# Five layer norms done in halves of 128 positions, in a chain of six layers on one core

## What is computed

```
y   = x + neighbourhood_attention(x) * gate(x)            # layer 0
a   = layernorm(y) * ln_g + ln_b                          # norm 1
xn  = group_norm(a);  t1 = xn + attention(xn)             # layer 1, softmax over 256 positions
x2  = layernorm(t1)                                       # norm 2
t2  = t1 + dilated_attention(x2)                          # layer 2
x3  = layernorm(t2)                                       # norm 3
t3  = t2 + top2_of_8_experts(x3)                          # layer 3
x4  = layernorm(t3)                                       # norm 4
t4  = t3 + causal_attention(x4)                           # layer 4
x5  = layernorm(t4)                                       # norm 5
out = t4 + lstm(x5)                                       # layer 5, 256 steps in sequence
layernorm(z) = (z - mean(z)) / sqrt(var(z) + 1e-5)        # over the 64 channels of a position
```

## Time and profile before

| | |
|---|---|
| Median of 3 runs | 422.7 us (421.83 to 422.84) |
| The profiled execution, its own time | 422.28 us |
| Its span, first to last instruction | 420.4 us |
| Busy: PE, DVE, ACT | 70%, 61%, 50% of the span |
| Mean granted TensorE clock | 0.635 of 2.4 GHz |
| LSTM loop, first matmul to the transposes of its result | 118.3 to 417.0 us |

### The profile page before, as it was taken

One profiled execution on the slowest core, in us unless ns is written; L12 is line 12 of the kernel. 1 busy time (PEld: TensorE's weight loads), 2 busy tenths in 40 slices (PEclk: granted clock), 3 DMA queues, 4 the chain that ended last, 5 costly groups with the idle time before them and its releaser, 6 DMA issues.

```text
span 420.4 us, 11844 instructions
## 1 busy us (share of the span) xinstructions
PE 292.6 (70%) x3273; PEld 224.5 (53%) x3278; DVE 257.7 (61%) x2308; ACT 212.3 (50%) x1172; POOL 12.1 (3%) x22
## 2 busy tenths in 40 slices
PE   6899889989875666666556666665566666656663
PEld 2466347743455555555555555555555555555553
DVE  1786454655356666666666666666666666666665
ACT  2687253254455555555555555555555555555552
POOL 5410000000000000000000000000000000000000
PEclk9999999799975555555555555555555555555555
DMA  7500000000000000000000000000000000000000
GB/s 278 229 3 2 0 2 1 0 2 0 0 3 2 0 0 0 0 0 0 0 0 0 0 0 0 0 0 0 0 0 0 0 0 0 0 0 0 0 0 12
DMA packets 2972, 5.60 MB, mean 13 GB/s; under 512 B 1424, under 2 KB 1680, under 8 KB 2960
## 3 DMA queue, kind: packets, MB, share of 16 engines
q1 hardware_dynamic: 2672, 5.09, 3.3%
q10 hardware_dynamic: 288, 0.36, 0.2%
HBM read 5.32 MB, written 0.13 MB: 13 GB/s over the span
## 4 chain that ended last, share of the span: by engine, by line
ACT 38%; PE 37%; DVE 14%; issue 9%; DMA 1%; SPq 0%; DVEq 0%
ACT bank L383 20%; PE bank L665 17%; ACT gi L371 10%; DVE ha L949 6%; DVE terms_a L949 4%; ACT bank L373 4%; PE bank L424 2%; PE bank L446 2%; PE bank L394 2%; PE bank L435 1%; PE bank L597 1%; PE bank L558 1%; PE bank L609 1%; DMA cst<-in_const 1%; PE bank L479 1%
## 5 line engine op out<-in xcount | busy, mean ns | idle before, releaser
L665 PE MATMUL bank<-ha,vparts 128*128 128x1 f16 x1536 | 96.0, 169 | 110.8 <-DVE ha L949 110.8
L665 PEld LDWEIGHTS bank<-ha,vparts 128*128 128x128 f16 x1536 | 75.1, 107 | 133.7 <-DVE ha L949 133.7
L371 ACT ACTIVATE gi<-bank 128x1 f32<-128x1 f32 x256 | 43.8, 171 | 145.4 <-PE bank L665 145.4
L383 ACT ACTIVATE bank<-bank,hc,gi 128x2 f32<-128x2 f32 x256 | 83.5, 326 | 0.0
L946 DVE TENSOR_SCALAR go<-go 128x1 f32<-128x1 f32 x256 | 39.4, 154 | 66.3 <-ACT go L377 66.3
L665 PE MATMUL bank<-hb,vparts 128*128 128x1 f16 x768 | 76.4, 165 | 0.0
L665 PEld LDWEIGHTS bank<-hb,vparts 128*128 128x128 f16 x768 | 60.7, 104 | 0.0
L949 DVE CUSTOM_DVE_ANT_0 terms_a<-bank,go 128x3 f32<-128x3 f32 x256 | 41.2, 161 | 29.2 <-ACT bank L383 0.2
L661 PE MATMUL bank<-x,w5s 128*128 (+1 forms) x198 | 56.0, 358 | 0.1
L474 PE MATMUL bank<-ones,w5s 128*128 128x8 f32 x198 | 55.6, 355 | 0.0
L955 DVE SCALAR_TENSOR_TENSOR cell<-bank,gi,hc 128x1 f32<-128x1 f32 x256 | 54.7, 214 | 0.0
(11 more groups left out here) (215 smaller groups left out, 293.6 us busy)
## 6 DMA issues: line engine op xcount, KB each, us to landing
rel<-in_positions SPq DMA_DIRECT2D x4, 352.0 KB, 5.4
w3s<-in_w SPq DMA_DIRECT2D x1, 804.0 KB, 9.6
ltr<-in_later SPq DMA_DIRECT2D x1, 709.0 KB, 7.3
w2s<-in_w SPq DMA_DIRECT2D x1, 640.0 KB, 8.4
w5s<-in_w SPq DMA_DIRECT2D x1, 576.0 KB, 10.6
w0s<-in_w ACTq DMA_DIRECT2D x1, 336.0 KB, 4.0
w1s<-in_w SPq DMA_DIRECT2D x1, 256.0 KB, 7.5
w4s<-in_w SPq DMA_DIRECT2D x1, 192.0 KB, 10.5
```

Source lines behind the costliest of these rows:

```text
L371: act.activation(gi[:], bank[pre + 1][:, at:at + 1], ACT.Sigmoid, scale=1.0 / PRE)
L383: act.activation(tc_ends, gt.broadcast_to([P, 2]), ACT.Tanh, scale=gi[:], bias=hc[:]).then_inc(on("tanh_c"), 1)
L665: return mm(bank[3 * parity + k][:, at:at + 1], vparts[:, part, k], h, start=False, stop=False, skip_group_check=True)
```

## The change

Every step of a norm is issued for columns 0 to 127 and then for columns 128 to 255, each with a semaphore count of its own, and the two halves have separate banks. The copy to `rsw` goes; in place of the transposes, four f32 matmuls take the reciprocals themselves as the stationary operand, repeated 64 times by a broadcast, against the identity. The sources are made in halves. Seven of the eight `keep_clock` matmuls of norms 1 to 4, and all of norm 5's, go. Norm 5's `b_part`s move ahead of it, in place of one of the fillers there, and the first `x_part`s wait for the first half of x5 alone, the loop for both. After the group norm's square root, ACT asks for the Exp table. The experts' gate takes the first half of x3 as soon as it is there.

```diff
-        dif_bank, var_bank, rs_bank = ({n: bank[3 * (n == 5) + i] for n in range(1, 6)} for i in (0, 1, 2))
+        norm_bank, var_bank = ({n: (bank[3 * (n == 5) + i], bank[3 * (n == 5) + i + 1]) for n in range(1, 6)} for i in (0, 2))
+        half = [slice(h * P, (h + 1) * P) for h in range(HALVES)]
...
                 ask_table(ACT.Sqrt)
+                first = HALVES * (n - 1)
+                for h in range(HALVES):
+                    act.wait_ge(on("dif_mm"), first + h + 1)
+                    act.activation(sq[:, half[h]], norm_bank[n][h][:, 0:P], ACT.Square).then_inc(on("squares"), 1)
                 act.wait_ge(on("eps_set"), 2)
+                for h in range(HALVES):
+                    act.wait_ge(on("var_mm"), first + h + 1)
+                    act.activation(sd[:, h], var_bank[n][h][:, 0:B], ACT.Sqrt, bias=epsc[:, 0:1]).then_inc(on("root"), 1)
...
             act.activation(gtm[:, 2:3], gtm[:, 1:2], ACT.Sqrt, scale=-1.0, bias=epsc[:, 1:2]).then_inc(on("gsd"), 1)
+            ask_table(ACT.Exp)
...
+            def norm(n, src, made):
+                first = HALVES * (n - 1)
+                for h in range(HALVES):
+                    pe.wait_ge(on(made), h + 1)
+                    mm(norm_bank[n][h][:, 0:P], c("centre"), src[:, half[h]], start=True, stop=True).then_inc(on("dif_mm"), 1)
+                for h in range(HALVES):
+                    pe.wait_ge(on("squares"), first + h + 1)
+                    mm(var_bank[n][h][:, 0:B], sq[:, half[h]], c("means"), start=True, stop=True).then_inc(on("var_mm"), 1)
+                for h in range(HALVES):
+                    pe.wait_ge(on("rs"), first + h + 1)
+                    pe.wait_ge(on("dif"), first + h + 1)
+                    for b in range(B):
+                        m = mm(norm_bank[n][h][b * C:(b + 1) * C, 0:P], rs[:, h, b:b + 1].broadcast_to([P, C]),
+                               ident, start=True, stop=True)
+                    m.then_inc(on("rs_mm"), 1)
                 if n < 5:
+                    keep_clock(var_bank[n][0], 1)
...
             for h in range(HALVES):
+                pe.wait_ge(on("x3"), (h + 1) * B)
                 for b in range(B):
                     u = h * B + b
                     m = mm(bank[2][:, u * E:(u + 1) * E], x3[:, b, h * P:(h + 1) * P], cols(w3s, W3, "gate"),
...
-            keep_clock(bank[1], 4)
-            pe.wait_ge(on("t4"), 1)
+            keep_clock(bank[1], 3)
             pe.wait_ge(on("ub_scaled"), 2)
             pe.wait_ge(on("ones_set"), 1)
-            norm(5, t4[:])
+            for k in range(3):
+                b_part(0, k)
+            norm(5, t4, "t4")
...
             for k in (1, 0, 2):
                 x_part(0, k, 0)
+            pe.wait_ge(on("x5"), HALVES)
...
+            for h in half:
+                link(stt(out=pg[:, h], in0=bank[1][:, h], scalar=v("bp0"), in1=gate[:, h], op0=ALU.add, op1=ALU.mult))
+                tt(y0[:, h], pg[:, h], xf[:, h], ALU.add).then_inc(on("y0"), 1)
...
+                for h in range(HALVES):
+                    dve.wait_ge(on("squares"), first + h + 1)
+                    dve.tensor_copy(dif[:, half[h]], norm_bank[n][h][:, 0:P]).then_inc(on("dif"), 1)
+                for h in range(HALVES):
+                    dve.wait_ge(on("root"), first + h + 1)
+                    dve.reciprocal(rs[:, h], sd[:, h]).then_inc(on("rs"), 1)
...
+                for h in range(HALVES):
+                    dve.wait_ge(on("rs_mm"), first + h + 1)
+                    dve.wait_ge(on("dif"), first + h + 1)
+                    if n == 3:
+                        for b in range(B):
+                            r = slice(b * C, (b + 1) * C)
+                            tt(dst[r, b, half[h]], dif[r, half[h]], norm_bank[n][h][r, 0:P], ALU.mult).then_inc(on(done), 1)
+                    else:
+                        tt(dst[:, half[h]], dif[:, half[h]], norm_bank[n][h][:, 0:P], ALU.mult).then_inc(on(done), 1)
...
+            for h in half:
+                stt(out=t1[:, h], in0=bank[2][:, h], scalar=v("bp1"), in1=xn[:, h], op0=ALU.add, op1=ALU.add)\
+                    .then_inc(on("t1"), 1)
...
+            for i, h in enumerate(half):
+                tt(cc[:, h], bank[5][:, h], wsig[:, h], ALU.mult).then_inc(on("cc"), 1)
+                dve.wait_ge(on("cc"), 2 + i)
+                tt(t4[:, h], cc[:, h], cc2[:, h], ALU.add).then_inc(on("t4"), 1)
```

More of the change, by code:

```diff
@@ L126, in build @@
         sd, rs = sb("sd", [P, HALVES, B]), sb("rs", [P, HALVES, B])
-        rsw = sb("rsw", [P, HALVES, B, C])
         epsc = sb("epsc", [P, 2])
@@ L475, in b_part @@
                           start=True, stop=False, skip_group_check=True)
-            def norm(n, src):
-                mm(dif_bank[n][:, 0:N], c("centre"), src, start=True, stop=True).then_inc(on("dif_mm"), 1)
-                keep_clock(rs_bank[n], 2)
-                if n < 5:
[L482 to L501, removed]
-            keep_clock(bank[1], 4)
+            def norm(n, src, made):
[13 more added lines that the diff above has]
+                    m.then_inc(on("rs_mm"), 1)
+                if n < 5:
+                    keep_clock(var_bank[n][0], 1)
+            norm(1, y0, "y0")
+            keep_clock(bank[4], 4)
             pe.wait_ge(on("gst"), 1)
@@ L506, in _ @@
             mm(bank[2][:, 0:2], c("group"), gst[:], start=True, stop=True).then_inc(on("group_mm"), 1)
-            keep_clock(bank[1], 7)
+            keep_clock(bank[4], 7)
             pe.wait_ge(on("xn"), 1)
@@ L543, in _ @@
             keep_clock(bank[6], 2)
-            pe.wait_ge(on("t1"), 1)
-            norm(2, t1[:])
-            pe.wait_ge(on("x2"), 1)
+            norm(2, t1, "t1")
+            pe.wait_ge(on("x2"), HALVES)
             pe.wait_ge(on("w2_in"), 16)
@@ L580, in _ @@
             keep_clock(bank[2], 2)
-            pe.wait_ge(on("t2"), 1)
-            norm(3, t2[:])
-            pe.wait_ge(on("x3"), B)
+            norm(3, t2, "t2")
             pe.wait_ge(on("w3_in"), 16)
             for h in range(HALVES):
+                pe.wait_ge(on("x3"), (h + 1) * B)
                 for b in range(B):
@@ L639, in _ @@
             down(E - 1)
-            pe.wait_ge(on("t3"), 1)
-            norm(4, t3[:])
-            pe.wait_ge(on("x4"), 1)
+            norm(4, t3, "t3")
+            pe.wait_ge(on("x4"), HALVES)
             pe.wait_ge(on("w4_in"), 16)
@@ L764, in _ @@
             dve.wait_ge(on("gate"), 1)
-            link(stt(out=pg[:], in0=bank[1][:, 0:N], scalar=v("bp0"), in1=gate[:], op0=ALU.add, op1=ALU.mult))
-            tt(y0[:], pg[:], xf[:], ALU.add).then_inc(on("y0"), 1)
+            for h in half:
+                link(stt(out=pg[:, h], in0=bank[1][:, h], scalar=v("bp0"), in1=gate[:, h], op0=ALU.add, op1=ALU.mult))
+                tt(y0[:, h], pg[:, h], xf[:, h], ALU.add).then_inc(on("y0"), 1)
             def norm(n, dst, done):
[L771 to L777, removed]
+                first = HALVES * (n - 1)
+                for h in range(HALVES):
[4 more added lines that the diff above has]
+                    dve.reciprocal(rs[:, h], sd[:, h]).then_inc(on("rs"), 1)
@@ L789, in _ @@
+            norm(1, lno, "lno")
+            dve.wait_ge(on("lno"), HALVES)
             ts(t0[:], lno[:], v("lng"), v("lnb"), ALU.mult, ALU.add).then_inc(on("t0"), 1)
@@ L825, in _ @@
             dve.wait_ge(on("proj1_mm"), 1)
-            stt(out=t1[:], in0=bank[2][:, 0:N], scalar=v("bp1"), in1=xn[:], op0=ALU.add, op1=ALU.add)\
-                .then_inc(on("t1"), 1)
-            norm(2, x2[:], "x2")
+            for h in half:
+                stt(out=t1[:, h], in0=bank[2][:, h], scalar=v("bp1"), in1=xn[:, h], op0=ALU.add, op1=ALU.add)\
+                    .then_inc(on("t1"), 1)
+            norm(2, x2, "x2")
             for d in range(3):
@@ L871, in _ @@
             dve.wait_ge(on("proj2_mm"), 1)
-            stt(out=t2[:], in0=bank[6][:, 0:N], scalar=v("bp2"), in1=t1[:], op0=ALU.add, op1=ALU.add)\
-                .then_inc(on("t2"), 1)
-            norm(3, x3[:], "x3")
+            for h in half:
+                stt(out=t2[:, h], in0=bank[6][:, h], scalar=v("bp2"), in1=t1[:, h], op0=ALU.add, op1=ALU.add)\
+                    .then_inc(on("t2"), 1)
+            norm(3, x3, "x3")
             dve.wait_ge(on("gate_mm"), 1)
@@ L918, in _ @@
             dve.wait_ge(on("down_mm"), E)
-            tt(t3[:], bank[7][:, 0:N], t2[:], ALU.add).then_inc(on("t3"), 1)
-            norm(4, x4[:], "x4")
+            for h in half:
+                tt(t3[:, h], bank[7][:, h], t2[:, h], ALU.add).then_inc(on("t3"), 1)
+            norm(4, x4, "x4")
             dve.wait_ge(on("w4_in"), 16)
@@ L937, in _ @@
             dve.wait_ge(on("x5_zero"), 1)
-            norm(5, x5[:, 0:N], "x5")
+            norm(5, x5, "x5")
             split = "ha holds at most 11 bits by its grid, hb is rounded as a rest"
```

9 lines of the change are left out of this document (removed).

## The result

The changed kernel takes 416.74 us (median of 20 runs, 415.36 to 421.31) and the kernel before 421.89 us (median of 20, 421.00 to 423.54). The medians are 5.2 us apart. The ratio is that of the means of all runs (417.67 and 422.06) and not of the medians: 0.9896, with a 95% interval of 0.9874 to 0.9918: 1.0% faster, 4.4 us. The forecast was 417.9 us, within 415.9 to 420.9, and 4.8 us of gain.

A forecast was written before the change was run, and what follows sets the result against it. The kernel was taken as bound by its unchanged LSTM loop (298.7 us) and the 118 us of serial layers before it. Terms summed to 4.77 us off 422.28, 417.51, plus 0.42 to the median: 417.9 us, range 415.9 to 420.9.

The forecast's parts named there:

- The chain of a norm: Second half of a norm, from the source's end to the result's: 2.69 us, against 3.63 before.
- The savings of norms 1, 2, 4 and 5: Norms issued by halves save 0.57 us in norm 1, 0.77 in norm 2, 0.83 in norm 4, 0.91 in norm 5.
- the Exp table: Layer 1: the table load moves into ACT's idle time, so the Exps start earlier; 0.45 us saved.
- the gate's term: After norm 3: the first half's four gate records run under DVE's products, saving 0.46 us.
- norm 3's: Two products per half, one per image: 4.08 us becomes 3.30, saving 0.78; 1.24 with the gate.
- Layer 2: The stage from x2 to t2, with no instruction changed: 0 us saved.
- rival C: The clock's fall at 72.4 goes, values' projections and transposes run faster, about 2.5 us: 415.4 us; chance 0.08.
- Rival A: Without fillers the clock falls in the norms: 420.9 us with one fall (chance 0.09), 426 with a long one (0.04).
- single fall: One clock fall in the norms costs at most 3.4 us, about 3 where PE isn't always the bound: 420.9; chance 0.09.
- Rival B: The norms' halves don't overlap; only the copy's 0.32 per norm and the Exp table remain, 2.05 us: 420.2; chance 0.13.

The follow-up runs named there:

- exp_only: The kernel before, with only the Exp table asked for right after the group norm's square root: 421.39 us, ratio 0.9988.
- whole_bcast: The kernel before, norms whole and fillers kept, with 64-wide broadcast-reciprocal matmuls replacing copy and transposes: 421.91 us, ratio 1.0002.
- fill_3: The changed kernel with the fillers put back in norm 3 alone: 417.46 us, ratio 0.9886.
- no_fill: The kernel before, norms whole, with only the change's reduced fillers (one at the end of norms 1 to 4, none inside): 426.23 us, ratio 1.0105.
- rs_turn: The changed kernel with fillers in norms 1 to 4, but with the copy to rsw and the transposes, by halves: 417.31 us, ratio 0.9888.
- logit_fill: The changed kernel with fillers in norms 1 to 4 and four more among layer 2's logits matmuls: 416.73 us, ratio 0.9882.

## Why the prediction came out right

**Its steps.** The chain of a norm was priced at 2.69 us and measured at 2.65. The savings of norms 1, 2, 4 and 5 and of the Exp table came within 0.12 us each, and the gate's term was shown by undoing it. In norm 1 the saving was 0.12 larger: y0's pair ends 1.26 us after pg's start (44.17 to 45.43), against 1.31 taken, and the chain behind it is 2.62, against 2.69. In norm 5 it was 0.12 larger as well, 0.10 of it because the squares begin 1.38 us after the first cc and not 1.48.

**The step that was mis-sized** is norm 3's: "0.20 because DVE is still at the first half's pair, 0.24 + 0.29 for the last two". It took the spacing of 0.22 to 0.24 that two products of 128 partitions have. The four products of 64 partitions take 1.24 us at 0.29 each, so they start 0.32 apart and don't overlap at all; at 0.24 apart they would have taken 1.01, which is 0.23 of the 0.27 that the term missed. The whole pair of before says the same, 0.87 for two of 0.42, and I had that row. The saving forecast for norm 3 was 0.27 too large.

**Layer 2 was put at nothing, for want of a sign in the trace, and gave 1.91 in this profile.** That is rival C in part: the low clock still came, but for 3.4 us. No term of the sum stands for it, and the profile of before from which the prediction started had the long form. It belongs to neither kernel alone. In the profiles of exp_only and whole_bcast, which are as slow as before, layer 2 takes 16.11 and 16.10 us, and in that of the changed kernel's upper group 17.75. Over all profiles it ranges from 15.51 to 17.75, with the place and length of the low stretch. So the single pair of profiles shows 6.9 us of gain where the medians show 5.2 and the ratio 4.4. That 4.8 lies between them is partly luck: the short low clock in layer 2 gives more than was forecast, the upper group takes it back. And 417.9 starts from 422.7, the median of three runs of before, where twenty give 421.89; from there the forecast would have been 417.1.

**Rival A was real, and its single fall was priced wrong.** The forecast held against it that in 88 to 90 us PE had little but gate matmuls and idle time "and the clock stayed at 1.00", and put a single fall at 420.9. Of the changed kernel's 26 runs, 7 to 9 lie at 419.5 to 421.3, and the two profiles in that range (this kernel's at 420.68 and fill_3's at 420.93) show extra falls together with the long form of layer 2.

That these runs lie where the prediction put a single fall is luck. It priced one fall at about 3 us, and an extra stretch of 3.4 us cost 1.08 us in the experts, 1.40 in norm 4 and layer 4, and 1.58 in layer 4; the group reaches 421 only with two of them, or with one and an early fall before the loop, and with 2.16 us from layer 2's long form and 0.6 to 1.1 us from the start.

The prediction gave single falls 0.09 and called itself wrong if a window of a norm or of the experts showed 0.50. By that sign it holds for the lower group alone: in the profile at 420.68 the clock is 0.50 in the experts (88 to 90) and in norm 4 (108 to 109). A clock low through all of the experts did not come.

no_fill shows what the fillers had been doing for the whole norms: without them its profile has three extra falls and the six runs are 4.1 us slower. The halves of the changed kernel, with the same fillers gone, mostly keep the clock. They shorten a norm to 2.65 us and put eight f32 records of 128 columns into it; which of the two does it was not separated.

Here the Trainium skill (TensorE: Matmul & The Clock Gate, HAM oscillation) had the right direction, that gaps between bursts of matmuls bring the throttle back; no_fill's windows at norms 1, 3 and 4 agree, 0.54 to 0.66 where before has 1.00. Gaps are not the whole condition: at layer 2 the clock of before fell after PE had been busy for 4.46 of 4.46 us (68.00 to 72.46). What the Trainium skill states of transposes (TensorE: Matmul & The Clock Gate, Part 4: PE-mode transpose), that they count less for the clock than matmuls, was not tested: rs_turn, with transposes and fillers, had no extra fall in its profile.

**Rival B fell.** The halves overlap on every engine in norm 2's rows, and the chain is 2.65 us, where rival B left it at 3.31. (Its time of 420.2 lacks the 0.42 between profile and median that the forecast has; with it, it is 420.7.)

**A version to use.** The changed kernel with the fillers in norms 1 to 4 has a median of 415.59 us over 12 runs, against 416.94 over the changed kernel's 26, and none of its runs is in the upper group. Most of that difference is the upper group. With the open points above on its slower runs and on the chips, it is the better version as far as was measured.

## What to carry to other kernels

Where one tile goes through three engines in turn, halves that follow each other hide part of every step whose time grows with the columns, here 0.74 us of 3.63 (rs_turn's norm 2; the broadcast gave 0.24 more), and a reader that needs only the first half should wait for that alone. A source made in halves ends later, here by 0.07 (t3) to 0.32 us (y0), and that comes off. Price the pieces by counting every record of the form that will run, with the number of partitions, and look whether two such instructions in the trace overlap at all. Dummy matmuls that nobody waits for may be what holds the clock; if they are removed with a change, run the kernel often enough to see a second group of times, and try the removal by itself.

## What the runs showed of the hardware that was not expected

- Two 64-wide f32 matmuls into partitions 0 and 64 with a broadcast reciprocal as weights cost 0.055 us a record of 128 columns, half of the 0.11 estimated for full width from the earlier trace rows: the repeated operand costs nothing that shows.
- Norm 3's DVE products on 64 partitions each, by turns on partitions 0 to 63 and 64 to 127, did not overlap (0.32 us apart at 0.29 each), while two on 128 partitions did (0.51 us for two of 0.29). Whether the partitions or the layout of x3 is the reason was not tried.
- PE busy without a gap did not keep the clock at layer 2: it was busy 4.46 of 4.46 us before the fall of before, and 10.99 of 11 before that in logit_fill. In all 13 profiles the fall comes during the tiny matmuls or at most 1.3 us behind them; that they are its cause is argued, no run takes them away.
- Two profiles of one kernel differ by 2.16 us in a stage with the same instructions (layer 2, 15.59 and 17.75), by where the low clock lies in it and whether it lasts 3.4 or 6.9 us.
